# Adapter rows of the second tile in a buffer of their own, the last B0 store moved in front, up rows loaded sooner, and mixing's split behind h3's

## The reference

```python
x = x + _L0(x, ids0, W, Wr, A, B)      # x@W.T + 2 * top-2 of 8 experts (rank 16)
x = x + _L1(x, ids1, weights)          # weights[ids1]: a 64x64 matrix over the sequence
x = x + _L2(x, A, B, ids2)             # (x @ B[id].T) @ A[id].T, 64 adapters, rank 16
x = x + _L3(x, ids3, W, b, lora_As, lora_Bs)   # x@W.T + b + 2*(x @ A[id]) @ B[id], 32 adapters
```

## Time and profile before

| | us |
|---|---|
| runs (three) | 869.48, 870.11, 870.61; median 870.11 |
| the profiled execution: its own time | 872.91 |
| its span in the trace | 871.1 |
| PE busy (share of the span) | 859.5 (99%) |
| DVE busy | 678.9 (78%) |
| ACT busy | 384.7 (44%) |
| POOL busy | 249.0 (29%) |

### The profile page before, as it was taken

One profiled execution on the slowest core, in us unless ns is written; L12 is line 12 of the kernel. 1 busy time (PEld: TensorE's weight loads), 2 busy tenths in 40 slices (PEclk: granted clock), 3 DMA queues, 4 the chain that ended last, 5 costly groups with the idle time before them and its releaser, 6 DMA issues.

```text
span 871.1 us, 15477 instructions
## 1 busy us (share of the span) xinstructions
PE 859.5 (99%) x4620; PEld 795.8 (91%) x4620; DVE 678.9 (78%) x1900; ACT 384.7 (44%) x859; POOL 249.0 (29%) x343
## 2 busy tenths in 40 slices
PE   9999999999999999999999999999999999999998
PEld 7788888888888889899999999999999999999997
DVE  5994545665474736699999999999999889999896
ACT  5663324444355723444534534534534435445343
POOL 2411000000001123532523524524415415325230
PEclk9999999999999999999999999999999999999999
DMA  8534697659688766556656656656656666566664
GB/s 317 193 97 133 166 252 195 186 191 336 218 270 241 159 167 158 166 165 176 201 176 181 193 175 195 200 170 190 207 153 190 186 180 191 168 187 193 176 188 147
DMA packets 120393, 166.24 MB, mean 191 GB/s; under 512 B 33142, under 2 KB 79990, under 8 KB 120310
## 3 DMA queue, kind: packets, MB, share of 16 engines
q1 hardware_dynamic: 120310, 165.26, 63.9%
HBM read 128.78 MB, written 42.73 MB: 197 GB/s over the span
## 4 chain that ended last, share of the span: by engine, by line
PE 86%; DVE 3%; DMA 3%; SPq 3%; POOL 2%; issue 1%; ACT 1%; DVEq 0%; POOLq 0%; ACTq 0%
PE ps_w L2155 14%; PE ps_d L2147 13%; PE ps_d L2155 11%; PE ps_o L2054 11%; PE ps_d L2076 10%; PE ps_o L2076 9%; PE ps_o L2168 5%; PE ps_d L2162 4%; PE ps_s L2054 3%; PE ps_o L2192 3%; PE ps_s L2198 1%; DMA mdraw<-t 1%; DMA CT_raw<-mov 1%; PE ps_w L2162 1%; DMA t<-md_main 1%
## 5 line engine op out<-in xcount | busy, mean ns | idle before, releaser
L1500 DVE TENSOR_TENSOR stat_lo<-stat_raw,stat_hi 128x512 fp32r<-128x512 f32 (+1 forms) x150 | 148.1, 1006 | 49.4 <-ACT stat_hi L1040 40.3
L1040 ACT ACTIVATE stat_hi<-stat_raw 128x512 fp32r<-128x512 f32 (+1 forms) x150 | 115.3, 789 | 67.0 <-DVE stat_raw L1518 39.8
L888 POOL TENSOR_TENSOR stat_raw<-stat_raw,ident 128x128 f32<-128x128 f32 x36 | 27.3, 761 | 256.8 <-DMA stat_raw<-stat 256.8
L933 POOL TENSOR_TENSOR w_lo<-mdraw,w_hi 128x512 fp32r<-128x512 f32 x32 | 41.4, 1295 | 162.7 <-ACT w_hi L1040 162.7
L2147 PE MATMUL ps_d<-w_hi,stat_hi 128*128 128x392 f32 x240 | 81.5, 340 | 0.7 <-issue 0.7
L2147 PE MATMUL ps_d<-w_hi,stat_lo 128*128 128x392 f32 x240 | 81.4, 339 | 0.0
L2147 PE MATMUL ps_d<-w_lo,stat_hi 128*128 128x392 f32 x240 | 81.3, 339 | 0.0
L2054 PE MATMUL ps_o<-chunk_hi,stat_hi 128*128 128x512 f32 x168 | 65.8, 392 | 1.1 <-DVE stat_lo L1500 1.1
L2054 PE MATMUL ps_o<-chunk_hi,stat_lo 128*128 128x512 f32 x168 | 65.4, 389 | 0.0
L2054 PE MATMUL ps_o<-chunk_lo,stat_hi 128*128 128x512 f32 x168 | 65.4, 389 | 0.0
L1040 ACT ACTIVATE rows_hi<-rows_raw 128x512 fp32r<-128x512 f32 x50 | 31.3, 627 | 56.2 <-DMA rows_raw<-u 28.1
(11 more groups left out here) (303 smaller groups left out, 2551.6 us busy)
## 6 DMA issues: line engine op xcount, KB each, us to landing
up<-tu SPq DMA_DIRECT2D x124, 256.0 KB, 4.2
stat_raw<-x SPq DMA_DIRECT2D x33, 512.0 KB, 3.4
mdraw<-t SPq DMA_DIRECT2D x124, 136.0 KB, 2.5
out<-outb SPq DMA_DIRECT2D x30, 512.0 KB, 4.3
stat_raw<-stat SPq DMA_DIRECT2D x52, 256.0 KB, 3.3
stat_raw<-stat SPq DMA_DIRECT2D x26, 512.0 KB, 4.9
rows_raw<-x SPq DMA_DIRECT2D x30, 256.0 KB, 3.3
chunk_raw<-mov SPq DMA_DIRECT2D x24, 256.0 KB, 5.9
```

Of the source, the lines that this page charges most:

```text
L888: return nc.gpsimd.tensor_tensor(out=own, in0=own, in1=ident[:, :], op=ALU.add)
L933: nc.gpsimd.tensor_tensor(out=lower_w, in0=rows, in1=upper_w.bitcast(F32), op=ALU.subtract).then_inc(pool_md, 1)
L1040: return nc.scalar.activation(dst, src, ACT.Copy)
L1500: return nc.vector.tensor_tensor(out=dst, in0=src, in1=rounded.bitcast(F32), op=ALU.subtract)
```

## The change

1. **Tile 1's rows get a place of their own.** `md_second` lies over `up2` and the start of `up3`, which are not yet in use. Tile 0 is now loaded whole (272 columns) into `mdraw`, tile 1 right behind it into `md_second`, and tile 2 into `mdraw` when tile 0 has been read. `md_at(t)` gives buffer and semaphore to ACT and POOL. The separate B0 load of tile 0 is gone.
2. **The last B0 store stands in front.** `store_mb(1)` is issued right behind the eight `md_main` stores, and tile 0's load waits for it too (`st_mb`), where before it stood behind tile 0's load.
3. **The up rows of tile 0** (`load_up2(0)`, `load_up3(0)`) move from `step(1)` into `first()`, between `load_s3(1)` and `load_x1(1)`, behind a wait until tile 1 has been read from `md_second`.
4. **POOL's order in `first`**: `place_b(0)` ahead of `place_w(1)`, and `place_b(1)` ahead of `mix_identity(0)`.
5. **Mixing's split in the loop**: `mix_hi(a)` and `mix_lo(a)` leave the end of `step` and stand in `fore` of the next couple, behind `h3_hi(b2)` on ACT and behind `h3_rows(b2)` on DVE.

```diff
+        md_second = placed(late_at, "md_second", [P, 2 * BT, FULL], F32)
...
-        b0_first = md_b0[1][:, 0:2 * BT, :]
...
+        def md_at(t):
+            return (md_second, ld_md_second, MD_LOADED) if at(t, 1) else (mdraw, ld_md, MD_LOADED * max(t, 1))
...
             def load_md(t):
...
-                sp.wait_ge(pool_mb, 2 * t)
-                sp.wait_ge(pool_ud, 2 * t)
...
+                if t > 0:
+                    front = 1 if at(t, 2) else t
+                    sp.wait_ge(pool_mb, 2 * front)
+                    sp.wait_ge(pool_ud, 2 * front)
+                md_rows(t, mdraw, ld_md)
...
+            store_mb(1)
             for made_c in D_CHUNKS:
                 sp.wait_ge(st_md[made_c], 16 * STORES)
             sp.wait_ge(st_own, 16 * OWN_STORES)
-            load_md_first(0, slice(0, MAIN_COLS.stop), mdraw[:, :, 0:MAIN_COLS.stop], ld_md)
-            store_mb(1)
             sp.wait_ge(st_mb, 16 * len(D_CHUNKS))
-            sp.wait_ge(pool_md, 1)
-            sp.wait_ge(pool_ud, 2)
-            load_md_first(1, slice(0, FULL), mdraw, ld_md)
-            load_md_first(0, B0_COLS, b0_first, ld_mb)
+            load_md(0)
+            md_rows(1, md_second, ld_md_second)
 
             def first():
+                load_md(2)
                 load_x0(1)
                 sp.wait_ge(pool_const, CONSTS)
                 load_mix(0, 0)
                 sp.dma_start(bias_row[:, :], bias3[None, :].to_broadcast([P, D])).then_inc(ld_once, 16)
                 load_s2(1)
                 load_s3(1)
-                load_md(2)
+                sp.wait_ge(pool_mb, 4)
+                sp.wait_ge(pool_ud, 4)
+                load_up2(0)
+                load_up3(0)
                 load_x1(1)
                 load_s4(1)
                 load_md(3)
 
             def step(j, fin):
                 a, b, a1, b1, b2 = numbers(j)
-                load_up2(a1)
                 if fin:
+                    load_up2(a1)
                     store_out(b2)
-                load_up3(a1)
+                    load_up3(a1)
...
                 place_w(0)
                 ud_lo(0)
+                place_b(0)
                 place_w(1)
-                place_b(0)
                 ud_lo(1)
+                place_b(1)
                 mix_identity(0)
-                place_b(1)
...
                 if fin:
                     h3_hi(b2)
+                    mix_hi(a1)
                     h3T_copy(b2)
...
                     h3_lo(b2)
                     h3_rows(b2)
+                    mix_lo(a1)
```

More of the change, by code:

```diff
@@ L422, in build @@
         st_md = [sem(f"st_md{c}") for c in D_CHUNKS]
-        ld_mb, st_mb = sem("ld_mb"), sem("st_mb")
+        ld_md_second, st_mb = sem("ld_md_second"), sem("st_mb")
+        MD_LOADED = 16 * 2 * BT
         st_rows = [sem(f"st_rows{n}") for n in range(4)]
@@ L625, in choose, with md_rows @@
                 chosen2[t], chosen3[t] = index(AD2, t, NE2), index(AD3, t, NE3)
-            def load_md(t):
-                sp.wait_ge(pool_mb, 2 * t)
-                sp.wait_ge(pool_ud, 2 * t)
[L631 to L640, removed]
+            def md_rows(t, rows, arrived):
+                for b in range(BT):
+                    sp.dma_start(rows[:, b, :], t2[chosen2[t][b]]).then_inc(arrived, 16)
+                for b in range(BT):
+                    sp.dma_start(rows[:, BT + b, :], t3[chosen3[t][b]]).then_inc(arrived, 16)
+            def load_md(t):
+                if t > 0:
[3 more added lines that the diff above has]
+                md_rows(t, mdraw, ld_md)
             def load_mix(t, turn):
@@ L928, in place_w @@
             def place_w(t):
-                pool.wait_ge(ld_md, 16 * 2 * BT * (t + 1))
-                rows = mdraw[:, :, MAIN_COLS].rearrange("p q (k r) -> p k q r", r=RANK)
+                raw, arrived, count = md_at(t)
+                pool.wait_ge(arrived, count)
+                rows = raw[:, :, MAIN_COLS].rearrange("p q (k r) -> p k q r", r=RANK)
                 upper_w, lower_w = [v[:, :, MD_AT:P_AT].rearrange("p k (q r) -> p k q r", r=RANK) for v in w]
@@ L935, in place_b @@
             def place_b(t):
+                raw, arrived, count = md_at(t)
+                pool.wait_ge(arrived, count)
                 if at(t, 0):
-                    pool.wait_ge(ld_mb, 16 * 2 * BT)
                     pool.wait_ge(st_md[1], 16 * STORES)
-                    rows = b0_first
                 else:
                     pool.wait_ge(pe_xp, t)
-                    rows = mdraw[:, :, B0_COLS]
+                rows = raw[:, :, B0_COLS]
                 upper_b, lower_b = [v[:, 0:MD].rearrange("p (q r) -> p q r", r=RANK) for v in b03]
@@ L948, in ud_lo @@
             def ud_lo(t):
+                rows, arrived, count = md_at(t)
+                pool.wait_ge(arrived, count)
                 for n, (first, dst) in enumerate(((0, u2s), (BT, d3m))):
-                    raw = mdraw[:, first:first + BT, OWN_COLS].rearrange("p b (k r) -> p b k r", r=RANK)
+                    raw = rows[:, first:first + BT, OWN_COLS].rearrange("p b (k r) -> p b k r", r=RANK)
                     pool.wait_ge(act_ud, 2 * t + n + 1)
@@ L1268, in md_hi @@
             def md_hi(t):
-                act.wait_ge(ld_md, 16 * 2 * BT * (t + 1))
+                raw, arrived, count = md_at(t)
+                act.wait_ge(arrived, count)
                 if t in (1, 2):
@@ L1274, in md_hi @@
                 round_to(w[hi][:, :, MD_AT:P_AT].rearrange("p k (q r) -> p k q r", r=RANK),
-                         mdraw[:, :, MAIN_COLS].rearrange("p q (k r) -> p k q r", r=RANK)).then_inc(act_md, 1)
+                         raw[:, :, MAIN_COLS].rearrange("p q (k r) -> p k q r", r=RANK)).then_inc(act_md, 1)
             def ud_hi(t):
-                act.wait_ge(ld_md, 16 * 2 * BT * (t + 1))
+                rows, arrived, count = md_at(t)
+                act.wait_ge(arrived, count)
                 if at(t, 0):
@@ L1462, in step @@
                 Lb_hi(j)
-                mix_hi(a)
             def last(j):
@@ L2002, in step @@
                 Rb_lo(j)
-                mix_lo(a)
             def last(j):
```

## The result

| | before | changed |
|---|---|---|
| median of six runs each | 870.57 us | 875.33 us |
| fastest to slowest | 869.48 to 870.88 | 874.43 to 876.36 |
| profiled execution: its time, its span | 872.91, 871.1 | 874.43, 872.7 |

The account below looks back on a forecast made before the run. PE was taken as the bound (busy 859.5 of 871.1 us), so only its idle time could be won: median 870.11 - 1.3 (transition) - 0.3 (late load in the loop) = 868.5 us, range 866.8 to 870.4.

Parts of the forecast that it names:

- Waits (1), (2), (3): PE's transition waits for w_lo of tile 1, b_lo of tile 1, w_lo of tile 2: 0.42, 0.33, 0.67 us, all to go.
- The B0 store in front: Tile 0's rows wait for this store, opening a new PE wait at `others(0)`: 0.9 us, ends 0 and 1.9.
- x1 behind the up rows: x1 queues behind 1 MB of up rows, lands at 354.0 (353.2 to 354.4); POOL's sums start then instead of at 355.03.
- the forecast's own chain: From x1's landing: sums start, h2_lo 7.3 us behind x1, PE at the copy ahead of T3 12.14 us after h2_lo.
- The up rows sooner, ahead of x1: Part on the up rows' earlier issue: no gain by itself, but they stand in the queue ahead of x1.
- PE's own way: PE's arrival at the copy ahead of T3: old 374.38 less five waits (2.59) plus the new one (0.9), 372.7.
- DVE's way: Arrival at the same place through h2_lo on DVE: 361.3 + 12.14 = 373.4; the later way counts, 1.3 us gained.
- Mixing's split: In the loop, moving it behind h3's puts 0.2 to 0.3 us in front of `Ra_raw`, hidden: cost 0.
- Rival (D): Slower: mix_lo becomes the bound in each of 14 couples, 14 x 0.29 = 4.1 us, less 1.3: 872.9; chance 0.05.
- The saving at couple 11: In the loop, PE's 1.11 us wait for h3T behind a late load goes; 0.3 us taken for the median.
- With the new wait at 1.9 as well, 0.5: Low end of the transition gain: x1 at 354.4 gives 0.9 us, and with a 1.9 us B0-store wait 0.5.

Follow-up runs that it names:

- the fastest version: Changed kernel, but tiles 0 and 1 without B0 columns before the B0 store, mixing split and x0 back, up rows behind tile 3's: 867.56 us, ratio 0.9966.
- the kernel in which POOL waits: The fastest version with the mixing split behind h3's and POOL waiting for that split ahead of its second sum: 867.43 us, ratio 0.9965.

## Why the prediction was wrong

**Waits (1), (2), (3): right.** All three are gone in the changed kernel, and in the fastest version PE is 1.3, 1.8 and 2.6 us ahead of the old execution at these places (0.6 of it from before the transition).

**The B0 store in front: right, a little small.** Taken: 7.5 us to its landing, rows of tile 0 from 328.0 on, a wait of 0.9. Measured: 7.9 us, 328.17, a wait of 1.12 and against the old execution 1.3 us lost. The estimate from the Trainium skill's page (DMA: Bandwidth & Descriptors) was 1.6 us for this store, and so 1.1 us less of wait. The trace doesn't agree: the store landed 3.2 us behind the last md_main store. The nearest row was the better guide. How much the store costs in runs was not isolated; it was always put back together with x0 behind the rows.

**x1 behind the up rows: the step that failed in the transition, right in its mechanism and mis-sized.** Taken: landing at 354.0, at the worst 354.4. Measured: 355.9 here, and in the four other profiles with a 1 MB load in front of x1 354.7, 358.1, 355.2 and 355.8. My sum took each of the four loads at the pace of the earlier trace rows, issue to the last landing, 6.7 us for 1 MB. In the changed kernel they are issued from 344.89 on behind the S blocks, land 5.1 to 7.8 us after their issue, and are through at 354.9. The bounds 353.2 to 354.4 left no room for loads that share the engines, nor for the scatter. With the measured landing the forecast's own chain comes out right: sums at 355.94, 7.54 and 12.14 us behind them 375.62, which is where PE starts. Instead of the 1.3 us of gain forecast at 374.71 that is 0.9 of loss, and 1.8 if the 0.9 us by which this execution was ahead of the old one before the transition are counted. What it does to PE: h2T 1.43 instead of the 0.7 that were left.

**x0: missed.** "The up rows sooner, ahead of x1" weighs one queue crossing, but `load_md(2)` crosses `load_x0(1)` as well, and that isn't in the sum. It was readable in the kernel before:

```profile
341.87 1.06 ACT L1040 ACTIVATE stat_hi<-stat_raw 128x1024 fp32r<-128x1024 f32 x1 [1.61 <-DMA stat_raw<-x]
```
```profile
342.97 1.23 DVE L1500 TENSOR_TENSOR stat_lo<-stat_raw,stat_hi 128x1024 fp32r<-128x1024 f32 x1 [2.38 <-ACT stat_hi L1040]
344.41 0.59 DVE L1902 TENSOR_TENSOR y_raw<-ps_d,part 128x416 f32<-128x416 f32 x1 [0.22 <-PE ps_d L2162]
```

x0's rounding on ACT began as it landed, and its split on DVE ended 0.2 us ahead of the `y_raw` that PE wants, while x0 now lands 2.0 us later. In the forecast's sum the 1.38 us would have made PE's own way 374.1 instead of 372.7, later than the 373.4 of DVE's way: a gain of 0.6 instead of 1.3, so it doesn't turn the sign alone. In the changed kernel it was covered by x1's landing, as the run with x0 first shows. On a version without other waits it costs 3.7 us.

**Mixing's split: the step that failed in the loop, put at 0 and measured at 1.5 us.** "Behind the turning it puts about 0.2 to 0.3 us in front of `Ra_raw`" took the duration of a split that meets no sum. It was 1.18 to 1.19 us in the new place. The row for this was in the forecast's own group: the earlier trace rows has a `mix_lo` of 1.18 us at 690.66, four times the 0.29 of the row ahead of it, and the text read it only as a late load. One of POOL's sums began at 690.39, 0.27 us before it. Rival (D) named the right place, `mix_lo` becoming PE's bound in each couple, at 0.05, but not the meeting with the sum: it set the deciding slack at 0.29 us, where the real slack is 1.3 us (that `y_lo` was done at 426.47 before, and PE took it at 427.78), less the handing over, and the real addition 1.27 us (428.76 less 426.47 and PE's shift of 1.02). So it came true by a narrow margin, at 0.1 us per couple rather than 0.29. "PE has no idle time there" only says that the old slack was positive. The sign named for it, idle time of PE in the loop, doesn't show it either: the loop became slower without any. Instead of 0 it costs 1.5 us on the old kernel and 2.3 on the fastest.

**The saving at couple 11: not shown.** The changed kernel's profile has no wait for h3T in the loop, but also no late load; no run here compares such loads. The 0.3 in the sum stays unsupported.

**The clock: not in the forecast at all.** It was at full speed throughout the one profile of before, and waits were priced at their length. In the changed kernel's own six runs it has no part (0.999 or 1.0 in each). Their median is 0.9 us above the profiled execution, and what these 0.9 us are is open; the scatter of x1's landing is the likeliest, but was only argued.

**A slip in the sum.** "With the new wait at 1.9 as well, 0.5" doesn't follow: PE's own way would then be 373.7, still earlier than the 373.8 of DVE's way, and the gain 0.9.

The difference of the profiled pair, by PE's lead over the old execution: slower start of the old one -0.9; B0 store +1.3; waits (1) to (3) -0.3, -0.5 and -0.8; x0 +1.6; h2T +0.5; loop +1.5; the old one's late load -1.4. Together +1.0, as PE's last matmul shows (866.77 and 867.79). The terms of the transition are what PE met on its way; what it comes to at 375.62 is set by x1. With the 0.5 of the tail the spans differ by 1.6 us.

## What to carry to other kernels

Before an instruction is moved to a place where another engine is busy, look for a row in which the two already met: the same operation with a duration far above its median is the price, and the slack behind it is what decides. A load that is moved ahead in a queue has to be held against every load that it passes, and 1 MB in front of x1 moved its landing by 5.3 us on the fastest version (350.5 to 355.8), where the forecast had taken 2.2 (351.8 to 354.0). To price parts of a change whose waits hide each other, first build the version in which none waits, then put them back one by one: there x0 cost 3.7 us, the up rows 7.3, the mixing split 2.3, while undoing x0 on the changed kernel showed nothing. Behind a late load, feed its measured landing into the chain first: if that gives the measured time, what stands in front of it was covered.

## What the runs showed of the hardware

**DVE beside POOL.** In the changed kernel all 14 moved `mix_lo` (two operands in SBUF) began while a POOL sum ran, and ended 0.14 to 0.19 us behind the end of that sum, as in the rows of the loop: sum 424.26 + 1.29 = 425.55, split 424.51 + 1.19 = 425.70. Eleven took 1.18 to 1.19 us; three that began near a sum's end took 0.29, 0.38 and 0.71. The 18 that began outside any sum took 0.27 to 0.29, and in the kernel before seven splits of 0.28 to 0.29 us had a sum begin 0.22 to 0.23 us behind their start: the one that runs already is not held. `y_raw` at 425.73, with one operand in PSUM, ran its usual 0.59 beside a sum. The Trainium skill (SBUF — State Buffer, "Who interferes with whom") states it so: a DVE instruction with two SBUF inputs contends with a GpSimd instruction that reads SBUF, and the order of issue decides who blocks. The trace agrees with both, and the kernel in which POOL waits shows it by intervention: 1.29 us at most without, 0.39 with.

**The clock and a wait.** PE's granted clock went from 1.0 to 0.5 (2.4 to 1.2 GHz) in four profiles, each time at a wait of PE. At the waits of 1.9 us (at `others(1)`) and, in the changed kernel with the up rows behind x1, of 1.5 us (for `y_raw`) it fell 0.3 and 0.15 us after PE had gone on. At those of 4.4 and 4.7 us (for h2T) it fell 0.4 and 1.2 us before PE went on. It stood there for 3.4 us, at the longest wait for 6.8. Behind the waits of 1.0 to 1.6 us in the other profiles, and behind the 2.0 us in the profile with x0 behind tile 2's rows, it did not fall: the length of the wait alone doesn't decide it, and what does was not tested. A stretch of 3.4 us costs PE 1.5 to 1.7 us more than the wait itself, that of 6.8 us 2.6. As an estimate, a mean clock of 0.998 is what one stretch of 3.4 us at half speed makes of a run (3.4 x 0.5 / 868), and 0.996 two.
